# A ring of four expert weight slots in both mixture layers, and the two loads of an expert asked for one tile apart

## The reference

```python
# layer 0: 16 routed experts, 4 of them per token, 512 -> 256 -> 512, 2 shared ones
for e in range(E):
    routed = routed + combine[:, e:e + 1] * _mlp(x, re_w1[e], re_b1[e], re_w2[e], re_b2[e])
# layer 1: 16 routed experts, 2 of them per token, 512 -> 768 (gate and up) -> 512, 1 shared one
he = jnp.einsum('nd,edh->enh', xf, expert_w1) + expert_b1[:, None, :]
te = swiglu5(he, ...)
oe = jnp.einsum('enh,ehd->end', te, expert_w2) + expert_b2[:, None, :]
y = jnp.einsum('ne,end->nd', cw, oe)
```

## Time and profile before

| | |
|---|---|
| median of 3 runs | 2342.08 us (2335.74 to 2342.43) |
| the profiled execution | 2335.63 us, its span 2333.8 us |
| PE busy over the span | 2161.1 us (93%) |
| POOL busy over the span | 309.7 us (13%) |
| routed tiles of layer 0, first matmul to last add | 832.1 to 1072.3 us |
| routed tiles of layer 1, first matmul to last add | 2071.8 to 2322.8 us |

### The profile page before, as it was taken

One profiled execution on the slowest core, in us unless ns is written; L12 is line 12 of the kernel. 1 busy time (PEld: TensorE's weight loads), 2 busy tenths in 40 slices (PEclk: granted clock), 3 DMA queues, 4 the chain that ended last, 5 costly groups with the idle time before them and its releaser, 6 DMA issues. The chain is left out here.

```text
span 2333.8 us, 26804 instructions
## 1 busy us (share of the span) xinstructions
PE 2161.1 (93%) x7344; PEld 1242.2 (53%) x7345; DVE 1004.2 (43%) x2731; ACT 507.6 (22%) x903; POOL 309.7 (13%) x393
## 2 busy tenths in 40 slices
PE   6998889999998989885999999999899999989997
PEld 3444444545355445554544378854488854545553
DVE  7966778401114622222043465412265413634443
ACT  2112131110103012223111154211244212201221
POOL 1200000000000046562300000000000010013443
PEclk9999999999999999998999999999999999999998
DMA  4003000000002258885000000010100002248773
GB/s 127 1 0 119 1 1 18 1 18 0 0 0 96 90 121 201 222 197 104 36 0 27 25 12 1 1 63 0 37 1 1 1 5 70 80 154 269 216 240 95
DMA packets 77202, 154.58 MB, mean 66 GB/s; under 512 B 10217, under 2 KB 21524, under 8 KB 77116
## 3 DMA queue, kind: packets, MB, share of 16 engines
q1 hardware_dynamic: 59452, 113.06, 14.7%
q0 software_dynamic: 17664, 40.43, 8.7%
HBM read 119.50 MB, written 36.18 MB: 67 GB/s over the span
## 5 line engine op out<-in xcount | busy, mean ns | idle before, releaser
L1918 PE MATMUL bank<-arena 125*125 125x257 f32 x1600 | 355.8, 383 | 4.8 <-DVE arena L1837 4.8
L1918 PEld LDWEIGHTS bank<-arena 125*125 125x125 f32 x1600 | 302.2, 189 | 60.5 <-DVE arena L1837 6.4
L2194 PE MATMUL bank<-arena 128*128 x832 | 258.9, 446 | 13.4 <-issue 6.6
L973 PE MATMUL bank<-arena 125*128 125x500 f32 (+1 forms) x720 | 253.5, 513 | 3.1 <-ACT arena L1002 2.3
L473 PE MATMUL bank<-arena 128*125 128x512 f32 x480 | 212.6, 592 | 2.2 <-PEq L319 2.2
L2194 PEld LDWEIGHTS bank<-arena 128*128 128x128 f32 x832 | 152.0, 193 | 109.7 <-issue 60.0
L1712 PE MATMUL bank<-arena 128*125 128x512 f32 x480 | 207.8, 593 | 1.0 <-PEq L409 1.0
L973 PEld LDWEIGHTS bank<-arena 125*128 125x128 f32 x720 | 135.5, 189 | 121.1 <-issue 109.7
L2214 PE MATMUL bank<-arena 128*128 x360 | 171.2, 604 | 6.2 <-ACT arena L2280 4.0
L2332 DVE TENSOR_TENSOR arena<-bank,arena 128x384 f32<-128x384 f32 (+1 forms) x104 | 51.7, 497 | 257.1 <-PE bank L2194 211.6
L1896 ACT ACTIVATE arena<-arena 125x625 f32<-125x625 f32 x160 | 134.5, 900 | 102.4 <-DVE arena L1837 102.2
(11 more groups left out here) (336 smaller groups left out, 2277.4 us busy)
## 6 DMA issues: line engine op xcount, KB each, us to landing
arena<-in_L_ffn_expert_w SPq DMA_DIRECT2D x16, 1536.0 KB
arena<-in_L_ffn_re_w SPq DMA_DIRECT2D x32, 512.0 KB
arena<-in_L_ffn_expert_w SPq DMA_DIRECT2D x16, 768.0 KB
arena<-in_L_mix_Wqkv SPq DMA_DIRECT2D x6, 1024.0 KB, 10.8
arena<-in_L_gnn_W SPq DMA_DIRECT2D x3, 2048.0 KB, 8.1
arena<-in_L_ffn_expert_b SPq DMA_DIRECT2D x16, 384.0 KB
token_rows<-arena SPq DMA_DIRECT2D x2, 2500.0 KB
arena<-in_L_gnn_W SPq DMA_DIRECT2D x3, 1024.0 KB, 5.5
```

What stands on the lines that cost most here:

```text
L973: last = pe.matmul(st.bank[4 + n % 4][:, 0:cn], h[s][:, f * P:(f + 1) * P], st.counts[:, s, c0:c0 + cn], start=(s == 0), stop=(s == NT - 1))
L1918: return pe.matmul(st.bank[n % OUTS][0:TS, 0:ONCOL], prob[:, u % 2, s, j * TS:(j + 1) * TS], st.slots[:, head + 1, s, :], start=(s == 0), ...
L2194: last = pe.matmul(st.bank[UP[b][h]][:, 0:WP], xt[b][:, k, :], rt.ring[:, bass.ds(r, 1), k * W + h * WP:k * W + (h + 1) * WP].rearrange("p ...
```

## The change

- Both rings have four places (`ring = 4` in each class). Expert e takes the place of e - 4. In both layers expert 3 needs no wait for a place, and is asked for when `stage_routed` starts.
- Layer 0: w1 and bias of e are asked for when the first tile of e - 3 starts its add (`add_begun` at `done_by[e - 4]`), w2 (and the attention weights behind it) one tile later.
- Layer 1: w1 and bias of e are asked for when the last tile of e - 4 has been multiplied, w2 when the first tile of e - 3 starts its add.
- `find_places` has three laps where it had five, so four small DVE operations fewer in each layer.

```diff
-RING_EXPERTS = 3
...
 class L0_EXPERTS:
-    slots, early = P, 3
+    slots, early, ring = P, 3, 4
...
 class L1_EXPERTS:
-    slots, early = P, 1
+    slots, early, ring = P, 1, 4
...
 def load_expert(sp, rt, kind, ins, e, between=lambda: None):
-    w1, w2, b1 = rt.slot_parts(rt.ring[:, RING_EXPERTS - 1 - e % RING_EXPERTS, :])
+    w1, w2, b1 = rt.slot_parts(rt.ring[:, kind.ring - 1 - e % kind.ring, :])
...
-            for r in range(RING_EXPERTS, NE, RING_EXPERTS):
-                link(dve.tensor_scalar(lap, expert_f, RING_EXPERTS - 0.5, -float(RING_EXPERTS), ALU.is_gt, ALU.mult))
+            for r in range(kind.ring, NE, kind.ring):
+                link(dve.tensor_scalar(lap, expert_f, kind.ring - 0.5, -float(kind.ring), ALU.is_gt, ALU.mult))
                 link(dve.tensor_tensor(expert_f, expert_f, lap, ALU.add))
...
             for e in range(kind.early, NE):
                 if e >= R:
                     done = sp.value_load(rt.done_by[0:1, e - R:e - R + 1], min_val=1, max_val=TILES + 1)
-                    sp.wait_ge(down_ready, done)
-                if e >= R and not SW:
-
-                    load_expert(sp, rt, kind, ins, e, lambda: sp.wait_ge(add_begun, done))
+
+
+                    sp.wait_ge(down_ready if SW else add_begun, done)
+                    load_expert(sp, rt, kind, ins, e, lambda: sp.wait_ge(add_begun, done if SW else done + 1))
                 else:
                     load_expert(sp, rt, kind, ins, e)
                 if mw is not None and e in MIX_AT:
                     mw.load(sp, MIX_AT[e])
```

More of the change, by code:

```diff
@@ L1093, in stage_experts @@
     SLOT = KT * W + F * D + W
-    rt.ring = ar.whole[:, ar.end - RING_EXPERTS * SLOT:ar.end].rearrange("p (r n) -> p r n", r=RING_EXPERTS)
+    rt.ring = ar.whole[:, ar.end - kind.ring * SLOT:ar.end].rearrange("p (r n) -> p r n", r=kind.ring)
     rt.slot_parts = lambda slot: (slot[:, 0:KT * W].rearrange("p (k n) -> p k n", k=KT),
@@ L1119, in stage_experts @@
     stage_front(nc, st, Arena(ar.whole, ar.at, ar.end - kind.early * SLOT), kind, ins, rt, fi)
-    stage_routed(nc, st, SplitArena(ar.whole, free or [(DYN, DYN + KT * NODES + NT * D), (ar.at, ar.end - RING_EXPERTS * SLOT)]),
+    stage_routed(nc, st, SplitArena(ar.whole, free or [(DYN, DYN + KT * NODES + NT * D), (ar.at, ar.end - kind.ring * SLOT)]),
                  kind, ins, rt, out, mw)
@@ L1443, in find_places @@
             link(dve.tensor_copy(rt.expert_of, expert_f))
-            for r in range(RING_EXPERTS, NE, RING_EXPERTS):
-                link(dve.tensor_scalar(lap, expert_f, RING_EXPERTS - 0.5, -float(RING_EXPERTS), ALU.is_gt, ALU.mult))
+            for r in range(kind.ring, NE, kind.ring):
+                link(dve.tensor_scalar(lap, expert_f, kind.ring - 0.5, -float(kind.ring), ALU.is_gt, ALU.mult))
                 link(dve.tensor_tensor(expert_f, expert_f, lap, ALU.add))
-            link(dve.tensor_scalar(expert_f, expert_f, -1.0, RING_EXPERTS - 1.0, ALU.mult, ALU.add))
+            link(dve.tensor_scalar(expert_f, expert_f, -1.0, kind.ring - 1.0, ALU.mult, ALU.add))
             link(dve.tensor_copy(rt.ring_of, expert_f))
@@ L2017, in stage_routed @@
     F, W, SW = kind.blocks, kind.w1_cols, kind.swiglu
-    R = RING_EXPERTS
+    R = kind.ring
     TILES = 2 * rt.most_pairs
```

## The result

The changed kernel takes 2350.06 us in the median of 4 runs (2347.08 to 2351.58), the kernel before in the same comparison 2340.63 us. The ratio is 1.0047, 95% interval 1.0035 to 1.0060. Forecast were 2339.3 us and a range that ends at 2350.0: the wrong sign, and 0.06 us outside.

A forecast was written before the change was run, and what follows sets the result against it. Layer 1 was taken as bound by PE, layer 0 by a chain through POOL and the DMA queues. Terms -2.3 + 3.6 - 3.6 + 0 - 0.5 gave -2.8 us: 2339.3 us against the median, range 2330 to 2350.

The forecast's parts named there:

- Layer 1, one expert sooner: Layer 1: w1 asked for 17 us sooner removes PE's two waits for weights, 0.64 and 1.65 us; -2.3 us.
- Layer 1, w2 later: Layer 1: w2 a tile after w1 adds a wait only in SP, and PE does not wait for gathers; 0.
- The first burst of layer 0: Layer 0, first add: 640 KB instead of 512 KB delays that add, +0.3 us for each of 12 experts; +3.6 us.
- The second burst: Layer 0: w2 at the second add frees the expert's end but follows the first burst closely; -0.5 and +0.2 each, -3.6 us.
- the two-tile expert: Layer 0, bursts 1.9 us apart: first two adds 4.50 us apart, not 3.55; taken as close bursts' price, +0.95 us an expert.
- The relief at an expert's end: Layer 0: without weights before the last add, an expert's end takes 5.77 us, not 6.59; up to -9.8 us for 12.
- The attention loads: Layer 0: moved with w2 to the second add, they may hide or catch a gather; 0, bounds -7.7 and +4 us.
- Expert 3 at the start: Layer 0: one expert's bursts move from the loaded stretch to the stage's beginning; -0.5 us.
- DVE: Both layers' fronts: four small operations fewer, 0.9 us, while PE is busy with shared experts; 0, at most -0.2 us.
- Rival C: Layer 0: the two bursts stack up, a gather is caught, POOL waits before the third add; +8.6 us, 2350.7 us, chance 0.17.
- The rule of the Trainium skill: DMA engines alternate between queues by packet, so burst placement in layer 0 would not matter; layer 0's burst steps 0 each.
- the row of 2.85 us: Layer 0, POOL's wait for an add two tiles back with an attention load behind w2; taken as 1536 KB's cost.

The follow-up runs named there:

- w2_third: Changed kernel, but layer 0's w2 and the attention load behind it wait until the third tile of e - 3 has been multiplied; ratio 1.0010 to before.
- attention_start_new: Changed kernel with all four attention loads asked for at the start of layer 0's routed stage; ratio 1.0024 to before.
- attention_start_old: New layer 1, old layer 0, with all four attention loads asked for at the start of layer 0's routed stage; ratio 0.9966 to before.
- ring4_old_moments: Changed kernel, four places kept, but layer 0's loads at the kernel before's moments within an expert; ratio 0.9994 to before.
- l1_only: Changed kernel with layer 0 put back to three places and the old load moments; 2333.24 us against 2336.75 before.
- w1_early_w2_second: Changed kernel with only layer 0's w1 and bias moved, to when the last tile of e - 4 is multiplied; ratio 1.0074 to before.
- attention_third: Changed kernel, but layer 0's four attention loads wait one add more, for the third add; ratio 1.0069 to before.
- after: The changed kernel itself, with the whole change, against the kernel before; 2350.06 us, ratio 1.0047.

## Why the prediction was wrong, step by step

1. *Layer 1, one expert sooner, -2.3 us:* right. Both waits are gone and measured alone this half is worth 3.5 us, of which the clock at the stage's end is a part (1.7 us in the profile) that the step did not foresee.
2. *Layer 1, w2 later, 0:* right, PE's windows are full.
3. *The first burst of layer 0, +3.6 us:* mis-sized; w2_third keeps that burst and has plain experts of 13.9 us: about 0.
4. *The second burst, -3.6 us:* this is the step that failed, in sign. It measured +10.1 us by the stages and 13.6 by the ratios, with the depth (attention_start_new against attention_start_old). The step priced the burst by how far it stood from the first one and left out that it catches a gather, which step 5 had thought of, though only for the four experts with an attention load. Its price, +0.95 us an expert from the two-tile expert in the earlier trace rows, was no price of bursts at all: the two adds of that expert stand 4.50 us apart in eleven of the twelve kernels, wherever the bursts lie, and the wait in that row is [1.26 <-issue]: the profile puts it down to no transfer. The same two adds in the changed kernel, with w1 asked for at 1042.81 and w2 at 1046.37:

```profile
1043.55 1.60 POOL L2118 DMA_INDIRECT token_sums<-arena  x1 [1.87 <-DMA token_sums<-arena]
...
1048.05 1.60 POOL L2118 DMA_INDIRECT token_sums<-arena  x1 [1.26 <-issue]
```

The right question was which transfer in flight POOL itself waits for next, and how soon. At the second add it is a gather started 1.5 us earlier (979.00 against 980.52); w2 comes 0.8 us after its start, and POOL is back for it 5.4 us after its start, at 984.38. At the first add, where w2 was before, there is a gather too, but w2 came 2.0 us after its start, and POOL was back only after 6.2 us and did not wait. The kernel before, with w2 at 979.98:

```profile
977.97 1.01 POOL L2110 DMA_INDIRECT arena<-token_rows,arena  x1 [2.10 <-DVE arena L2326]
...
984.16 0.19 POOL L2098 COPY arena<-arena 128x1 int32 x1
```

None of the rows I had chosen showed a gather. The relief at an expert's end did come: in the changed kernel the add at 976.97 follows the one before it by 5.78 us, as in the earlier trace rows without weights. But it is 0.8 us, and the third add of that kernel's plain experts comes 5.7 to 6.4 us after the second and not 4.06.
5. *The attention loads, 0 with +4 as the upper bound:* +5.1 us by the stages (6.4 less 1.3), just above the bound that the step had itself worked out from a caught gather, and about +1 us by the ratios (5.4 less 4.4). Which it is stays open.
6. *Expert 3 at the start, -0.5 us:* wrong in sign as far as it can be told; ring4_old_moments against l1_only shows +1.6 us in the stage and +2.1 in the total, where the intervals overlap. About 1 us of it is the first matmuls, 5.48 us and not 4.42.
7. *DVE, 0:* nothing in the runs contradicts it.

Rival C, the two bursts stack up, had the right sign and the right wait: a gather is caught and POOL stands before the third add. The nearness of its total, 2350.7 us against 2350.06, is luck. Its price for layer 0, 11.4 us against 15.5 measured, comes from the two-tile expert, whose 0.95 us no burst made; layer 1's gain was larger than thought, and the median it counted from, 2342.08, lay 1.4 us above that of the comparison. Its name was not right: w1_early_w2_second shows that one burst is enough. It got a chance of 0.17 because weights at the old moments seemed to cost nothing (14.2 against 14.3 us an expert). That comparison takes one expert of each kind; the expert before the second one, with no load asked for in it either, took 13.3 us (1037.50 to 1050.79). And it could only say that the old moments were harmless, and nothing about others.

The rule of the Trainium skill that the forecast weighed (DMA: Bandwidth & Descriptors, Queues, rings and completion order: the engines take turns between queues) would have put layer 0 at no change. The runs do not test the turns themselves, but they contradict what the forecast drew from them, that the place of a burst does not matter: the same bytes at other moments made layer 0's stage 15.0 us longer with three places. The size of the burst counts less than the row of 2.85 us had suggested: at the same four experts 512 KB cost POOL waits of 1.7 to 2.4 us at the copy and 1536 KB 2.3 to 2.85 (attention_third and after).

## What to carry to other kernels

Before a load is moved, write down for its new moment which small transfers have just been started or are about to be, who waits for them next, and how long after their start. A load may be big where all that is in flight has slack, and not right beside a gather that an in-order engine soon waits for. Before a row is taken as the price of something, look whether the same interval is there where that something is missing. Deeper rings help where a wait for weights can be seen, as in layer 1; where none could be seen, as in layer 0, moving the requests only changed what they collided with.

## What the runs showed of the hardware

The moment of a 512 KB load within a period of some 14 us is worth 1.6 us of that period, with the same bytes on the same queues: asked for 0.7 to 1.1 us before the second add, a plain expert takes 15.5 us, asked for 1.4 to 2.2 us after it, 13.9 (after and w2_third).

The first twelve matmuls of layer 0's stage took 5.48 us in all eight kernels that asked for loads at the stage's start, and 4.38 to 4.44 us in the four that did not. The granted clock of the window 834 to 838 was 0.50 of full in the eight, which is the lower of the two levels, and 0.64 to 0.85 in the four, where PE went over to full clock within the window; PE had done little but 8 short matmuls in the 7 us or so before, in all of them. What ties a load to that clock the runs do not show. It is part of the price of asking for expert 3, or for the attention weights, there.
